# Tropical maximum of a graph network's feed-forward: a re-ordered first pass, slots by separate halves of the columns, and a steeper base of the test

## The reference, cut to what matters

```python
t = jnp.max(xx[:, None, :] + Wt[None, :, :], axis=-1) + bt   # xx [tokens, 256], Wt [1024, 256]
```

## Time and profile before

| | us |
|---|---|
| median of 3 runs | 7198.53 (7197.23 to 7199.57) |
| the profiled execution, its own time | 7195.66 |
| its span, first to last instruction | 7193.9 |
| mean granted clock of PE | 0.967 of full speed |

### The profile page before, as it was taken

One profiled execution on the slowest core, in us unless ns is written; L12 is line 12 of the kernel. 1 busy time (PEld: TensorE's weight loads), 2 busy tenths in 40 slices (PEclk: granted clock), 3 DMA queues, 4 the chain that ended last, 5 costly groups with the idle time before them and its releaser, 6 DMA issues. The chain is left out here.

```text
span 7193.9 us, 107569 instructions
## 1 busy us (share of the span) xinstructions
PE 6380.4 (89%) x31084; PEld 4414.3 (61%) x31084; DVE 5517.3 (77%) x9823; ACT 3380.7 (47%) x6149; POOL 1740.0 (24%) x3907
## 2 busy tenths in 40 slices
PE   9989999999888836888888877888877799999999
PEld 6659999999877734555555554555444344444444
DVE  8983333333488886888888888999998799999998
ACT  6652222222244414555555552222211577777786
POOL 3320000000044414555555541122356000000000
PEclk9999999999899978999999998999999899999999
DMA  4430000000154422111111111012244222222211
GB/s 137 136 119 1 0 0 0 0 0 0 43 154 152 154 89 81 66 65 65 65 65 65 65 62 32 33 62 75 96 152 163 91 74 76 78 80 76 80 66 59
DMA packets 355974, 517.50 MB, mean 72 GB/s; under 512 B 27392, under 2 KB 297344, under 8 KB 355840
## 3 DMA queue, kind: packets, MB, share of 16 engines
q1 hardware_dynamic: 322944, 400.58, 17.2%
q0 software_dynamic: 32896, 115.51, 4.8%
HBM read 294.20 MB, written 221.79 MB: 72 GB/s over the span
## 5 line engine op out<-in xcount | busy, mean ns | idle before, releaser
L1788 DVE SCALAR_TENSOR_TENSOR t_tout<-t_fetched,t_top,t_tout 128x1024 f32<-128x1024 f32 x896 | 1145.1, 1278 | 242.6 <-PE t_fetched L1703 232.5
L1703 PE MATMUL t_fetched<-t_wpart,t_onehot 128*128 128x512 f32 x4096 | 1181.6, 416 | 160.2 <-DVE t_tout L1788 143.1
L2055 PE MATMUL ts_fetched<-t_wpart,ts_onehot 128*128 128x512 f32 x3232 | 991.6, 434 | 162.3 <-DVE ts_tout L2131 106.8
L1703 PEld LDWEIGHTS t_fetched<-t_wpart,t_onehot 128*128 128x128 f32 x4096 | 700.8, 188 | 513.9 <-DVE t_tout L1788 341.6
L580 PEld LDWEIGHTS l_ps<-hx,l_whh 128*128 128x128 f32 x8192 | 962.8, 193 | 16.8 <-DVE hx L521 3.7
L580 PE MATMUL l_ps<-hx,l_whh 128*128 (+1 forms) x8192 | 950.8, 275 | 3.2 <-DVE hx L521 3.2
L2131 DVE SCALAR_TENSOR_TENSOR ts_tout<-ts_fetched,ts_top,ts_tout 128x1024 f32<-128x1024 f32 x716 | 919.2, 1284 | 26.8 <-PE ts_fetched L2055 0.6
L2055 PEld LDWEIGHTS ts_fetched<-t_wpart,ts_onehot 128*128 128x128 f32 x3232 | 576.0, 197 | 494.7 <-DVE ts_tout L2131 388.3
L545 ACT ACTIVATE l_act<-l_ps 128x128 f32<-128x128 f32 x1024 | 284.1, 278 | 1054.2 <-PE l_ps L580 1054.2
L2559 DVE SCALAR_TENSOR_TENSOR f_line<-f_hinge,f_vec,f_line 128x1024 f32<-128x1024 f32 x512 | 656.8, 1283 | 63.0 <-ACT f_hinge L2443 48.9
L2027 ACT ACTIVATE ts_dist<-ts_index,t_pminus 128x512 f32<-128x512 f32 x202 | 139.3, 690 | 978.1 <-PE ts_index L2045 943.9
(11 more groups left out here) (370 smaller groups left out, 10723.1 us busy)
## 6 DMA issues: line engine op xcount, KB each, us to landing
t<-t_tout SPq DMA_DIRECT2D x128, 512.0 KB, 2.6
f_t<-t SPq DMA_DIRECT2D x64, 1024.0 KB, 5.2
g_adj<-in_adj SPq DMA_DIRECT2D x128, 256.0 KB, 3.0
g_adjt<-in_adjt SPq DMA_DIRECT2D x128, 256.0 KB, 2.7
t_x<-x_normalised SPq DMA_DIRECT2D x130, 128.0 KB, 2.3
g_x<-in_x SPq DMA_DIRECT2D x64, 256.0 KB, 2.8
x_kept<-g_x SPq DMA_DIRECT2D x64, 256.0 KB, 2.2
g_x<-x_kept SPq DMA_DIRECT2D x64, 256.0 KB, 2.8
```

The costliest lines, as they stand in the source:

```text
L1703: mm = pe.matmul(fetched[c % RING][:, h * CH:(h + 1) * CH], one_hot[g][:, c % GRP * P:(c % GRP + 1) * P], w_part[part][:, k, h * CH:(h + 1 ...
L1788: dve.scalar_tensor_tensor(t_out[j][:, :], column[:, :], value, t_out[j][:, :], ALU.add, ALU.max)\
L2055: mm = pe.matmul(fetched[buf][:, h * CH:(h + 1) * CH], one_hot[b][:, c % GRP * P:(c % GRP + 1) * P], w_part[part][:, k, h * CH:(h + 1) * C ...
```

## The change

It has three parts. (1) The first pass runs in another order: on DVE `best` and `find` stand together at the head of a tile, `name` behind use 1, and `test` handles tile s - 2 in place of s - 1 and stands behind use 2. On PE `turn_fall` is cut into two parts and `add_up` into four, laid between single fetches, the last two parts of `add_up` in the next tile. ACT takes `begin` ahead of `turn_hot`, and the copy of the turned powers (L1647) behind `count`; `allowed` gets a second buffer. POOL does `taken` and `next_best` ahead of `leave`, and `lift` ahead of the bound's inputs. Four tiles in place of two stand ahead of the loop. (2) Each half has its own plan and its own run of the slot stage: slots in order of that half's open columns, with g candidates of one half (not 4g of both); `CLASSES` are now numbers of candidates. y is gathered in rows of 512 bytes, and one copy names the rows of three DMAs. (3) `STEEPEST` is 40.

```diff
-CLASSES = (8, 4, 3, 2, 1)
+CLASSES = (16, 8, 6, 4, 3, 2)
-STEEPEST = 24.0
+STEEPEST = 40.0
...
-        tropical_slots(nc, v, left_dram, t_dram)
+        for k in range(KD):
+            tropical_slots(nc, v, k, left_dram, t_dram)
...
 (first pass, ScalarE)
             def slot(s, j):
+                begin(s, j)
                 turn_hot(G * s + 1, 1)
-                begin(s, j)
                     fall_off(s - 1, 1 - j)
                     count(s - 2, j)
+                    turned_fall(s - 1)
                 turn_hot(G * s + 2, 0)
...
 (first pass, TensorE)
                 spread(s, j, 1)
-                for c in range(4):
-                    fetch(s, c)
-                    turn_fall(s - 1)
-                for c in range(4, 6):
-                    fetch(s, c)
-                    add_up(s - 1, 1 - j)
+                fetch(s, 0)
+                    add_up(s - 2, j, 2)
+                fetch(s, 1)
+                    add_up(s - 2, j, 3)
+                fetch(s, 2)
+                fetch(s, 3)
+                    turn_fall(s - 1, 0)
+                fetch(s, 4)
+                    turn_fall(s - 1, 1)
+                fetch(s, 5)
                 spread(s + 1, 1 - j, 0)
-                for c in range(6, 8):
-                    fetch(s, c)
+                fetch(s, 6)
+                    add_up(s - 1, 1 - j, 0)
+                fetch(s, 7)
+                    add_up(s - 1, 1 - j, 1)
...
 (first pass, VectorE)
+                best(s + 1, 1 - j)
+                find(s + 1, 1 - j)
                 use(s, j, 1)
-                best(s + 1, 1 - j)
+                name(s + 1, 1 - j)
                 use(s, j, 2)
-                find(s + 1, 1 - j)
-                use(s, j, 3)
-                name(s + 1, 1 - j)
-                for c in range(4, CANDS):
+                    test(s - 2, j)
+                for c in range(3, CANDS):
                     use(s, j, c)
-                    test(s - 1, 1 - j)
...
 (plan, VectorE)
-                then(dve.max(sorted_key[:, eight], src[:, :]))
-                then(dve.match_replace(left_key[:, :], sorted_key[:, eight], src[:, :], -1.0))
+                for k in range(KD):
+                    last = dve.max(sorted_key[:, k, eight], src[:, k, :])
+                then(last)
+                for k in range(KD):
+                    last = dve.match_replace(left_key[:, k, :], sorted_key[:, k, eight], src[:, k, :], -1.0)
+                then(last)
...
 (slots, GpSimd, for each slot s)
-                    held(2, selected, s + 2)
-                    y_gather(s + 3, 1 - j, s + 4)
-                    held(3, fetched_used, RING + GRP * (s * g + base) + 1)
-                    t_gather(s + 2, j, s + 3)
-                    pool.tensor_copy(t_to[j][:, :], to_all[:, ds(s, 1)]).then_inc(to_named, 1)
-                    held(4, fetched_used, RING + GRP * (s * g + base) + GRP * g)
-                    held(5, to_named, s + 1)
+                    held(0, fetched_used, RING + first + j * g + 1)
+                    pool.tensor_copy(now[j][:, :], rows[:, ds(s + 3, 1), :].rearrange("p o n -> p (o n)"))\
+                        .then_inc(now_named, 1)
+                    held(1, now_named, s + 1)
+                    t_gather(j, now[j][:, 1:2])
+                    y_gather(1 - j, now[j][:, 0:1])
+                    held(2, fetched_used, RING + first + j * g + g)
                     pool.indirect_dma_start(t_dram, ...)
...
 (slots, VectorE, for each slot)
-                    select(i + j + 1, 1 - j, (i + 2 * j) * 8 + 16, 2 if g > CAND // 2 else 1)
-                    for c in range(g * GRP):
-                        use(first, i + j, j, g, j * g * GRP + c, (i + 2) * 8)
+                    select(i + j + 1, 1 - j, (i + 2 * j) * 8 + 16, 2 if g > CAND else 1)
+                    for c in range(g):
+                        use(first, j, g, c, (i + 2) * 8)
```

More of the change, by code:

```diff
@@ L1524, in tiles @@
         def tiles(eng, slot, last):
-            for s in range(2):
-                slot(s, s)
-            with eng.Fori(1, TILES // 2) as i:
+            for s in range(4):
+                slot(s, s % 2)
+            with eng.Fori(2, TILES // 2) as i:
                 for j in range(2):
@@ L1674, in last @@
                 fall_off(TILES - 1, 1)
[L1675 to L1676 removed]
+                count(TILES - 2, 0)
+                turned_fall(TILES - 1)
+                count(TILES - 1, 1)
             turn_hot(0, 0)
@@ L1722, in add_up @@
+            def add_up(s, j, part):
+                if part == 0:
+                    pe.wait_ge(fall_t_ready, s + 1)
+                    wait_past(pe, tested, s)
+                for u in range(2 * part, 2 * part + 2):
                     mm = pe.matmul(ps_sum[:, j, :], fall_t[:, u, :], exp_w[:, u, :], start=(u == 0), stop=(u == FT8 - 1))
-                mm.then_inc(summed, 1)
+                if part == 3:
+                    mm.then_inc(summed, 1)
             def slot(s, j):
-                before = not isinstance(s, int) or s > 0
+                one_back = not isinstance(s, int) or s > 0
+                two_back = not isinstance(s, int) or s > 1
@@ L1744, in _ @@
+                fetch(s, 7)
+                if one_back:
+                    add_up(s - 1, 1 - j, 1)
+            def last():
+                for part in range(2, 4):
+                    add_up(TILES - 2, 0, part)
+                for part in range(2):
+                    turn_fall(TILES - 1, part)
+                for part in range(4):
+                    add_up(TILES - 1, 1, part)
             spread(0, 0, 0)
@@ L1945, in tropical_slots @@
+        now = [sb(f"now{j}", [P, 3], I32) for j in range(2)]
+        index = [ctx.enter_context(nc.psum_tensor(f"ts{half}_index{b}", [P, GRP * P], F32)) for b in range(2)]
+        fetched = [ctx.enter_context(nc.psum_tensor(f"ts{half}_fetched{r}", [P, FFN], F32)) for r in range(RING)]
+        ident_b, w_part = v["ident_b"], v["w_part"]
+        bounds, rows = v["bounds"][half], v["rows"][half]
+        left_rows = left_dram[0:TOK + P, :].rearrange("t (k d) -> (t k) d", k=KD)
         y_in = [sem(f"y_in{j}") for j in range(2)]
@@ L2077, in _ @@
-            spread(0, 0, 0, 0)
+                    for r, n in enumerate(sizes):
+                        q = j * len(sizes) + r
+                        b = q % 2
+                        pe.wait_ge(one_hot_ready, hot + q + 1)
+                        for c in range(n):
+                            if c == 2:
+                                spread_next(i, j, r, b, sizes)
+                            fetch(first, j * g + r * GRP + c, 2 * g, b, c)
+                        if n <= 2:
+                            spread_next(i, j, r, b, sizes)
```

377 lines of the change are left out of this document (189 added, 188 removed).

## The result

| | before | after |
|---|---|---|
| median of 4 runs each | 7199.0 us (7197.23 to 7199.57) | 6724.34 us (6722.01 to 6724.77) |
| the profiled execution, its own time | 7195.66 us | 6724.72 us |
| its span | 7193.9 us | 6722.9 us |
| mean granted clock of PE | 0.967 | 0.959 |

The ratio is 0.934, with an interval of 0.9324 to 0.9357: 475 us faster. Forecast were 6790 us and a range of 6725 to 6885.

The account below looks back on a forecast made before the run. DVE was taken to bound the slots, with DVE and PE balanced in the first pass apart from DVE's waits on fetches. First pass -104, slots -321, plan +16 sum to -409 us: 6790 us, range 6725 to 6885.

Parts of the forecast that it names:

- the first pass: First pass: re-ordering cuts a tile from 12.0 to 11.15 us, 104 us less in all; ends nothing and 154.
- allowance for PE: First pass: cycle laid out as 11.07 us, taken as 11.15 because fetches 6 and 7 are only just ready.
- floor: First pass: PE's work per tile, summed from its rows, is 10.8 us and the cycle's lower limit.
- The slots: Slot stage: 502 uses in 128 slots, second start included, 898 us for 1219, so 321 less.
- The plan: Plan: 16 sort rounds with a second MAX8 and MATCH_REPLACE8, plus wider steps, 16 us more (8 to 25).
- Landings bind the light slots: Light slots: scatter landing takes twice as long, 5.3 us a slot, +53 us, 6843; chance 0.20.
- PE's clock: Slots: PE at 1.2 GHz makes light slots 5.0 us of PE's work, perhaps heavier ones too; 6823 to 6904; chance 0.08.
- POOL hidden: Light slots: POOL's gaps vanish and slots run at DVE's 3.84 us, -44 us, 6746; chance 0.10.
- The new order only moves the wait: First pass: interleaved parts cost PE restarts, tile stays near 11.7 us, 70 us of gain lost, 6860; chance 0.13.
- The base does nothing: Slots: the steeper base saves nothing, 38 candidates and 4 slots stay, +55 us, 6845; chance 0.03.
- slower than before: Light slots: the two buffer sets don't overlap, 13.1 us a slot, +568 us, 7358; chance 0.02.
- The feed-forward: Feed-forward behind the slots: stays as it was, no change in time.

Follow-up runs that it names:

- find_back: The changed kernel with DVE's best and find back between the uses, name and the test behind use 3; 6801.76 us.
- parts_whole: The changed kernel with PE's turning and sum of the test's powers in one piece each, in their old places; 6805.86 us.
- one_part: The changed kernel with first-pass fetches of two matmuls instead of four, lower part of the weights left out; 6684.9 us.
- eight other programs: Eight test kernels with the same slots as the changed kernel, edited or padded elsewhere; their slots took 881.3 to 883.9 us, against 898.6.
- y_by_act: The changed kernel with the slots' y loaded by plain DMAs from ACT's queue, always the first 128 tokens, instead of POOL's gather; 6693.56 us.
- pad_8: The changed kernel with 8 tiny DVE memsets, and a tile to hold them, added to the constants; 6720.73 us.

## Why the prediction was right in sign and low in size

**The step that failed** is the first pass: "12.0 - 11.15 = 0.85, times 126 tiles" gave 104 us, and 154 came. The mechanism was as told: both waits went, by the edits named for each (find_back, parts_whole). The term was mis-sized: a tile gained 1.21 (12.01 to 10.81) and not 0.85, 45 of the 50 us over the 126 tiles. The rest is the 3 us for two more tiles in flight, which didn't come (from the last tile's first use to the plan 19.3 us, for 20.3 before), and rounding. By parts of the cycle, means of tiles 21 to 120:

| part of the cycle | forecast | measured | why |
|---|---|---|---|
| end of use 7 to use 1 | 1.45 | 1.33 | as before: the quarter of `add_up` ahead of fetch 1 adds nothing, and the 1.38 of the tile in the earlier trace rows is above the mean |
| use 1 with `name` | 1.40 | 1.33 | `name` starts before use 1 ends |
| use 2 with the test | 1.72 | 1.53 | the test adds 0.21, not its 0.42 |
| the other five | 6.50 | 6.61 | 1.32 each |
| allowance for PE | 0.08 | in the rows above | PE's 0.19 (one_part) is 0.11 in the first row, the rest in small steps |

The first three are one mistake: I added durations as if nothing overlapped. On DVE a short step begins under the tail of the long one ahead of it; on PE the shown length of a matmul is more than its share of the pipeline. The row for DVE was in hand: in the earlier trace rows the test starts at 3522.64 and the use before it ends at 3522.72. The "floor" of 10.8 by PE was a coincidence: the cycle reached 10.81, but by DVE, which needs 10.6 with half the fetching.

**The range** failed by a step of its own. The text named 154 as the far end of this term, by the same sum of PE's work, and then let the lower bound take only 20 of the 50 between 104 and 154. With the end itself it would have been 6790 - 44 - 50 = 6696. That the median lies only 0.7 us below the stated range is chance: the first pass and the reloads were 63 us better than told, with neither of them in the lower bound at its size.

**The slots** came within 4 us, in part by luck: 502 uses in 128 slots, 895.3 forecast without the first start and 898.6 measured. The agreement hides errors that cancel. Where nothing is late a light slot follows POOL's cycle of 4.35, not 4.5; with the longer ones among them the average is 4.71 in after and 4.43 to 4.48 in the eight other programs, where 4.5 would be right to some 4 us. The start of the second half was forecast at 29.5, or 33.3 with the last slot of two (3.84) in it; from that slot's first use to the next half's first are 29.88, 3.5 less, though DVE's 16 loads into registers took 10.02 where 9 took 5.99. The other programs' 883 lie 12 under the forecast; these two parts make 7 of them, and the rest is not attributed. After's late signals of PE add 16. Slots of three and four run near DVE's pace as told, 5.20 and 6.40 on average (4.98 to 5.97 and 6.30 to 6.64).

**The plan** cost 14.5 with the first start, 18.7 forecast. A round of the sort is 1.17 as worked out (4156.33 to 4157.50 between two rows of MAX8); the steps behind it overlap, as on DVE elsewhere.

**The rivals.** *Landings bind the light slots*: the mechanism is there (24.7 us of waits for landings in the stage), the price isn't. The scatter issued at 4732.61 for 1.00 let the use at 4736.26 go, 2.65 behind its end, where the earlier trace rows have 2.43: landings didn't double at 236 GB/s. *PE's clock*: it fell, to a mean of 0.70 to 0.86 in windows of the light slots, by going back and forth between 2.4 and 1.2 GHz (1.00 and 0.50 in the rows above). Even at the lower level the two fetches of a slot, 3.78, and its `spread`, 0.44, are 4.2 us of PE's work, within POOL's 4.35, where the rival had reckoned with 5.0. A slot at that level can still be longer, since its fetches wait for ACT's one-hot matrices as well: the one from 4671.75 to 4676.94 us took 5.20. But averages of 4.43 to 4.48 leave room for few of these; a part of the open 16 us may be the clock's. The Trainium skill ("TensorE: Matmul & The Clock Gate", section "HAM oscillation — how this bites in real kernels") says that bursts with waits between them are throttled again and again. The trace agrees with it (0.50, then 1.00, and 192 us at the lower level in all); the price of the rival it doesn't bear out. *POOL hidden*: no; even with one of POOL's three DMAs taken off (y_by_act) a light slot is 4.20 and not 3.84. *The new order only moves the wait*: no wait over 0.15 us is left in the first pass but one of 4.5 and one of 4.9 at its head, and what PE still adds is 0.19 a tile. *The base does nothing*, *slower than before*: no.

**The feed-forward** was costed at nothing, since its instructions are the same. They are, but with the reloads 12 us went.

## What to carry to other kernels

Take the price of a step from the distance between starts, with and without it, and not from its duration; a floor that is a sum of durations is none, as here on DVE behind long operations and on PE. To learn what a second engine adds, halve its work and see what is left of the cycle: here 0.19 of 10.81, which no list of waits over 0.15 us shows. Where a far end of a term has been worked out, the range has to reach it. And before a few tenths of a per cent are put down to an edit, look whether a stage that the edit doesn't touch has moved as well: here two of them moved by 10 to 12 and by 15 to 17 us for 8 to 24 memsets elsewhere.

## What I had not expected of the hardware

- A 128x256 step of 0.41 us behind a 128x1024 one of 1.28 costs DVE 0.21; two such steps in a row lie 0.33 apart.
- The four matmuls of a fetch are shown as 1.19 us long, and PE's next matmul starts 1.02 behind their start.
- In the light slots PE's granted clock goes back and forth between 1.00 and 0.50: 192 of 899 us at the lower level, two fetches in 3.78 us there and in 2.13 at the upper one.
- A block of a loop of the same instructions takes 95.6 to 96.4 us with 0 to 3 packets on q14, or 98.1 to 98.6 with 4 to 9 (after, before, pad_8), and which of the two changed with eight memsets in another stage.
- POOL pauses 2.7 to 3.0 us ahead of the gather of t, three times in each of the five traces looked at, and once, of 2.26, where y's gather is taken off it.
- One stage of the same instructions and data took 898.6 us in one program and 881.3 to 883.9 in eight others, mostly by signals of PE that come up to 2.4 us behind the shown end of its matmuls; the cause is open.
